# One core, two interleaved lanes: another table of turns for a two-layer decoder in fp32

## The chip, the cores and the metric

The kernel runs on one core of a Trainium2 chip. The metric is the device time of one execution in microseconds. The kernel before has a median of 643.53 us over 3 runs (643.41 to 644.73). The profiled execution is a separate one, of 639.99 us.

The core's engines each take their own list of instructions strictly in order and meet only at semaphores: PE (matmul), DVE (vector), ACT (activation functions and copies), POOL (elementwise, here softmax scaling and parts of the expert product) and SP (issues the DMAs).

## The reference

`x` is (4, 256, 128), the context `ctx` is (4, 256, 128), all fp32. Six pre-norm residual stages:

```python
x = x + L0_attn(layernorm(x))        # 16 heads of 8; attn = softmax(q k^T * 128**-0.5) + rel_bias; out = layernorm(attn v)*gamma + beta
x = x + L0_xattn(layernorm(x), ctx)  # 16 heads of 64, causal and padding mask, keys and values from ctx
x = x + L0_ffn(layernorm(x))         # 8-bit activations, ternary weights, 128 -> 512, conv over 3 tokens, silu, 512 -> 128
x = x + L1_attn(layernorm(x))        # grouped heads, causal, scores + slope*(j - i), softmax, projection
x = x + L1_xattn(layernorm(x), ctx)  # per token: softmax over the 16 heads of k against the 16 heads of q
x = x + L1_ffn(layernorm(x))         # 8 experts of 128, top 2, plus one shared expert

def swiglu(h):                       # in L1_ffn, a = swiglu(h1 * h3), y = a @ w2.T + b2, weighted by the router
    g = jnp.minimum(h[..., ::2], LIMIT)
    l = jnp.clip(h[..., 1::2], -LIMIT, LIMIT)
    return g * jax.nn.sigmoid(ALPHA * g) * (l + 1.0)
```

## The kernel before, in words

The four batches of 256 tokens are split in two lanes, A (batches 0 and 1) and B (batches 2 and 3). A lane has its own half of the on-chip memory, its own four PSUM banks (`A_banks`, `B_banks`) and its own tiles, so the lanes share no data but weights. Each lane does the six stages one after another. In names the stages are `l0a` (`rel_attention`), `l0x` (`cross_attention`), `ffn` (`quantized_ffn`), `l1a` (`alibi_attention`), `l1x` (`head_attention`) and `moe` (`expert_ffn`). `A_l0a_xn` is thus lane A's normalized x of the first stage.

A stage gives, for each engine, a Python generator: the code between two `yield`s emits a few instructions with their semaphore waits. `course()` strings a lane's six generators together for one engine. `merged()` then takes from the two lanes, and from two helper programs, by a string of turns: "A4 W1 A3" takes four pieces of lane A's program, one of W's, three of A's. W is `weight_levels()`, which rounds the ffn weights to their levels and multiplies two projection matrices; it works in lane B's memory before B starts. L (`late_loads()`) issues, on SP alone, the loads of the last two stages' weights. There is one string for each engine, in the table `TURNS`. So the strings fix how A's and B's instructions alternate in each engine's list; the order within a lane is fixed by the generators, and what waits for what by the semaphores.

The lines that the prediction speaks of:

- Stage `l0a`: L439 loads the context (SP); L608 transposes it (PE); L148 to L155 take the statistics of x and L164 normalizes it (DVE), L159 is the power -0.5 between them (POOL); L172 transposes the result (PE); L493 copies that out of PSUM (ACT); L622 projects one tile of 128 tokens to q, k, v (PE). q and k are split in three bf16 parts, L541 and L544 on DVE, L462, L465 and L471 on POOL, into a stack `expT` that L637 transposes (PE) and L434 copies to `qkT` (DVE). POOL's memsets L452 to L457 clear a lane's stack and value tiles. L226 makes scores for the row maximum (PE), L299 takes it (DVE, `nmax`). L323 and L327 and the DMA of L252 (`shiftT` into `qkT`) put the maxima into the queries; then L262 and L263 make the scores again (PE).
- Stage `l0x`: for a pair of heads L950 to L954 make scores (PE), L879 their maxima (DVE), L803 the exponentials (ACT), L966 transposes them (PE), L820 copies them (ACT), L979 multiplies by the values (PE).
- `l1a` also projects the context for `l1x` (L1518, L1523, PE).
- Stage `l1x`, once for each eighth of the tokens: L1707 and L1714 copy operands out of PSUM (ACT), L1742 and L1747 take maximum and difference (DVE), L1718 the exponential (ACT), L1759 the sum (DVE), L1830 the next products (PE).
- Stage `moe`, once per expert and lane: L2054 the two hidden products (PE), L1950 a bias add (ACT), L2021 to L2036 the clamped product (DVE), L1956 the sigmoid (ACT), L1926 and L1932 the products with router weight and gate (POOL), L2086 the output product (PE). L2007 and L2067 prepare router weights; L2046 adds the result to x at the end (DVE).

The sigmoid and the exponential of ACT lie in different function tables. An `ACT_TABLE_LOAD` stands in ACT's list wherever the next function needs another table than the last did; where that is depends on the order of the lanes' instructions.

The functions that make and use the table:

Of the kernel before, what the change touches and what calls it, by code (L numbers as in the profile page):

```python
# [2343 lines left out]
def course(lane, name, eng):  # L2344

    for st in lane.plan:
# [9 lines left out]

TURNS = {
    "tensor":
# [7 lines left out]
    "vector":  # L2366
# [8 lines left out]
    "scalar":  # L2375
# [4 lines left out]
    "gpsimd":  # L2380
        "A12 B3 A4 B13 A10 B2 A2 B3 A4 B1 A1 B1 A1 B1 A2 B1 A1 B2 A2 B1 A1 B7 A3 B2 A3 B2 A1 B8 A8 B3 A3 B3 A1 B1 A2 B3 A1 B2 A2 B2 A2 B1 A10 B4 A1 B10 A1 B2",
    "sync":
        "A1 W13 B1 A2 B2 L1 A6 L1 A3 B7 A1 B3 A2 B2 A1 B1",
}


# [153 lines left out]
```

## Time and profile before

| | before |
|---|---|
| median of 3 runs | 643.53 us |
| the profiled execution | 639.99 us |
| its span, first to last instruction | 638.0 us |
| PE busy | 542.6 us (85%) |
| DVE busy | 421.6 us (66%) |
| ACT busy | 327.5 us (51%) |
| POOL busy | 193.3 us (30%) |
| mean granted clock of PE | 0.946 of full |

The span is what the records cover; 1.99 us of the profiled time lie outside it. The busy time of an engine is the part of the span in which it executes something. No engine is busy throughout, so an average says little: for each stretch one has to see which engine has no gaps and, where all have, what each gap waits for. The profile's timeline gives for each row the start and the time in us, the operation with the tile it writes and those it reads, how many like it follow one another, and in brackets how long the engine was idle just before and what released it ("1.18 <-DVE A_l0a_qkT L434": idle for 1.18 us until the DVE instruction of L434 had written that tile). The granted clock tells which of its two levels, 1.2 and 2.4 GHz, PE ran at: 1.00 is 2.4 GHz, 0.50 is 1.2 GHz, and a value between them is a mean over time at either.

### The profile page before, as it was taken

To read this page: it belongs to the slowest core of one execution; us is meant where nothing else is said; L and a number is where in the kernel's file an instruction comes from. 1 tells how busy PE (TensorE), PEld (TensorE's weight loads), DVE (VectorE), ACT (ScalarE), POOL (GpSimd) and SP (SyncE) were. 2 spreads that over 40 slices of the span, in tenths; PEclk is the share of its full clock that TensorE was granted. 3 is DMA by queue.
4 is the path that set the end of the run, shared out by engine and by line. 5 is a ranking of instruction groups with operands and counts; after the bars stand their busy time and mean duration, and the time that the engine had idled before them with its cause. 6 is when DMAs were issued, how large, how long until landed. Compare 5 with 4: busy or idle time off the path is not lost. (4 is left out here: it accounts for less than half of the span.)

```text
span 638.0 us, 12873 instructions
## 1 busy us (share of the span) xinstructions
PE 542.6 (85%) x4890; PEld 334.9 (53%) x4890; DVE 421.6 (66%) x1037; ACT 327.5 (51%) x809; POOL 193.3 (30%) x288
## 2 busy tenths in 40 slices
PE   1777888999999999778896479988997989999995
PEld 1533344344555656455464355665665766655553
DVE  5595674642563554788559865757556567689894
ACT  1424355556577574586642535553664547363440
POOL 3554200312263443332620031001113122335663
PEclk9875799999999999889998789999998999999997
DMA  8600000000030000000166005300000000300301
GB/s 289 258 2 2 2 3 3 1 3 2 1 134 0 2 1 1 2 2 1 43 174 234 1 2 165 103 3 2 4 3 2 3 3 1 134 2 0 133 2 33
DMA packets 25815, 27.92 MB, mean 44 GB/s; under 512 B 18177, under 2 KB 22794, under 8 KB 24858
## 3 DMA queue, kind: packets, MB, share of 16 engines
q1 hardware_dynamic: 25754, 27.10, 12.7%
q8 instruction: 39, 0.64, 0.4%
q14 instruction: 22, 0.18, 0.1%
HBM read 22.14 MB, written 4.75 MB: 42 GB/s over the span
## 5 line engine op out<-in xcount | busy, mean ns | idle before, releaser
L785 POOL TENSOR_TENSOR A_l0x_prob<-A_l0x_prob,A_l0x_inverted_sums 128x256 f32<-128x256 f32 (+1 forms) x32 | 26.2, 840 | 61.7 <-DVE A_l0x_inverted_sums L896 61.7
L785 POOL TENSOR_TENSOR B_l0x_prob<-B_l0x_prob,B_l0x_inverted_sums 128x256 f32<-128x256 f32 (+1 forms) x32 | 27.1, 868 | 46.6 <-DVE B_l0x_inverted_sums L896 46.5
L879 DVE TENSOR_REDUCE A_l0x_nmax<-A_banks 128x2 f32<-128x256 f32 (+1 forms) x32 | 16.3, 551 | 26.9 <-PE A_banks L954 26.9
L2054 PE MATMUL A_banks<-A_moe_xT,w_moe_rows 128*128 128x512 f32 x72 | 34.0, 599 | 0.0
L2054 PE MATMUL B_banks<-B_moe_xT,w_moe_rows 128*128 128x512 f32 x72 | 33.3, 599 | 0.0
L299 DVE TENSOR_REDUCE B_l0a_nmax<-B_banks 128x2 f32<-128x512 f32 x32 | 21.4, 686 | 17.4 <-PE B_banks L226 17.3
L299 DVE TENSOR_REDUCE A_l0a_nmax<-A_banks 128x2 f32<-128x512 f32 x32 | 21.4, 685 | 12.0 <-PE A_banks L226 11.8
L333 ACT ACTIVATE A_l0a_expT<-A_banks 128x512 f32<-128x512 f32 x32 | 18.5, 599 | 21.0 <-PE A_banks L263 21.0
L803 ACT ACTIVATE B_l0x_prob<-B_banks,B_l0x_nmax 128x128 f32<-128x128 f32 x64 | 26.0, 421 | 6.0 <-DVE B_l0x_nmax L879 6.0
L803 ACT ACTIVATE A_l0x_prob<-A_banks,A_l0x_nmax 128x128 f32<-128x128 f32 x64 | 26.0, 427 | 1.2 <-DVE A_l0x_nmax L879 1.2
L820 ACT ACTIVATE B_l0x_probT<-B_banks 128x384 f32<-128x384 f32 x32 | 15.8, 493 | 21.0 <-PE B_banks L966 21.0
L333 ACT ACTIVATE B_l0a_expT<-B_banks 128x512 f32<-128x512 f32 x32 | 19.1, 604 | 14.3 <-PE B_banks L263 13.9
L820 ACT ACTIVATE A_l0x_probT<-A_banks 128x384 f32<-128x384 f32 x32 | 15.8, 493 | 15.8 <-PE A_banks L966 15.6
L333 ACT ACTIVATE A_l1a_expT<-A_banks 128x384 f32<-128x384 f32 x32 | 15.5, 493 | 16.2 <-PE A_banks L266 16.0
L1683 POOL TENSOR_TENSOR A_l1x_prob<-A_l1x_prob,A_l1x_rz 128x512 f32<-128x512 f32 x8 | 8.3, 1043 | 49.9 <-DVE A_l1x_rz L1764 49.9
L1950 ACT ACTIVATE A_moe_h<-A_banks,w_moe_rest_rows 128x512 f32<-128x512 f32 x18 | 12.3, 684 | 20.9 <-PE A_banks L2054 20.9
L333 ACT ACTIVATE B_l1a_expT<-B_banks 128x384 f32<-128x384 f32 x32 | 15.2, 493 | 13.0 <-PE B_banks L266 12.8
L879 DVE TENSOR_REDUCE B_l0x_nmax<-B_banks 128x2 f32<-128x256 f32 (+1 forms) x32 | 16.2, 547 | 8.3 <-PE B_banks L954 8.3
L299 DVE TENSOR_REDUCE B_l1a_nmax<-B_banks 128x2 f32<-128x512 f32 (+1 forms) x24 | 16.3, 685 | 7.3 <-PE B_banks L234 7.2
L1950 ACT ACTIVATE B_moe_h<-B_banks,w_moe_rest_rows 128x512 f32<-128x512 f32 x18 | 12.3, 682 | 15.4 <-PE B_banks L2054 15.3
L2054 PEld LDWEIGHTS B_banks<-B_moe_xT,w_moe_rows 128*128 128x128 f32 x72 | 12.6, 190 | 13.3 <-issue 10.3
L966 PE MATMUL B_banks<-w_const_rows,B_l0x_prob 128*128 128x128 f32 x96 | 17.2, 290 | 2.1 <-ACT B_l0x_probT L820 1.7
(610 smaller groups left out, 1605.1 us busy)
## 6 DMA issues: line engine op xcount, KB each, us to landing
w_toeplitz_rows<-in_toeplitz_rows SPq DMA_DIRECT2D x1, 3072.0 KB, 15.8
w_moe_rows<-in_moe_rows SPq DMA_DIRECT2D x1, 2304.0 KB, 8.8
w_l1x_rows<-in_l1x_rows SPq DMA_DIRECT2D x1, 2048.0 KB, 8.6
A_l1x_values<-A_l1a_v_tokens SPq DMA_DIRECT2D x4, 512.0 KB, 3.2
A_l1x_v_groups<-A_l1x_values SPq DMA_DIRECT2D x16, 128.0 KB, 3.1
B_l1x_values<-B_l1a_v_tokens SPq DMA_DIRECT2D x4, 512.0 KB, 3.4
B_l1x_v_groups<-B_l1x_values SPq DMA_DIRECT2D x16, 128.0 KB, 3.3
w_l0x_vo_rows<-in_l0x_vo_rows SPq DMA_DIRECT2D x1, 1024.0 KB, 8.9
```

The lines of the kernel that those rows point to most:

```text
L299: dve.tensor_reduce(out, scores, AX, ALU.max, negate=True).then_inc(self.s_mx.sem, 1)
L333: act.activation(self.expT[:, u % self.ring, :], self.exp_bank(u)[:, 0:self.W], ACT.Exp, scale=self.scale).then_inc(self.s_p.sem, 1)
L785: ins = pool.tensor_tensor(pair, pair, bcast(rz[:, g % 2, i, :], 2, n), ALU.mult)
L803: ins = act.activation(prob[:, u % RING, at:at + n], bank[u % 2][:, at:at + n], ACT.Exp, bias=nmax[:, b, i, h:h + 1], accum_out=zsum[:, g ...
L820: act.activation(probT[:, u % 4, :], bank[2][:, 0:W], ACT.Copy).then_inc(s_pt.sem, 1)
L879: ins = dve.tensor_reduce(nmax[:, b, i, 2 * c:2 * c + 2], lane.banks[:, 0:2, at:at + n], AX, ALU.max, negate=True)
L966: ins = pe.transpose(bank[2][:, c * P:(c + 1) * P], prob[:, u % RING, c * P:(c + 1) * P], w["ident"][:])
L1683: pool.tensor_tensor(pr, pr, bcast(rz[:, n % 2, :], BL, 64), ALU.mult).then_inc(s_pn.sem, 1)
L1950: act.activation(h1[:, n % 2, :], hidden_bank(2 * n)[:, :], ACT.Identity, bias=w["moe_b1"][:, e, part:part + 1]).then_inc(s_h1.sem, 1)
L2054: pe.matmul(hidden_bank(k)[:, :], w["moe_w3" if which else "moe_w1"][:, ORDER[i], part, :], xT[:], start=True, stop=True).then_inc(s_h.sem, 1)
```

## The change

All five strings of `TURNS` are replaced, and nothing else. The generators, the waits, the tiles and the number of PE, DVE, POOL and DMA instructions stay as they are. ACT's list has eight table loads in place of ten, since in two places the functions of one table now stand together. Two of the five strings, with their old forms:

```diff
     "gpsimd":
-        "A12 B3 A4 B13 A10 B2 A2 B3 A4 B1 A1 B1 A1 B1 A2 B1 A1 B2 A2 B1 A1 B7 A3 B2 A3 B2 A1 B8 A8 B3 A3 B3 A1 B1 A2 B3 A1 B2 A2 B2 A2 B1 A10 B4 A1 B10 A1 B2",
+        "A11 B1 A3 B1 A1 B1 A1 B13 A10 B1 A2 B3 A2 B1 A2 B1 A1 B1 A1 B1 A2 B1 A1 B2 A2 B1 A1 B6 A1 B2 A1 B1 A4 B2 A1 B8 A8 B2 A2 B2 A1 B2 A2 B2 A1 B3 A1 B1 A1 "
+        "B1 A1 B1 A5 B1 A6 B1 A1 B12 A1 B1 A1 B2",
     "sync":
-        "A1 W13 B1 A2 B2 L1 A6 L1 A3 B7 A1 B3 A2 B2 A1 B1",
+        "W4 A1 W9 B1 A2 B2 L1 A6 L1 A3 B5 A1 B5 A2 B2 A1 B1",
```

In SP's list the first DMA before is lane A's context (L439), ahead of the constants and of A's x. After, it is the seventh, right behind B's x.

On POOL, in the first stage, where lane A splits its third and fourth tile of q and k (L462 to L471) and lane B's part begins (L159 and the memsets), the order before is:

```order
L465 TENSOR_TENSOR A_l0a_split<-A_l0a_rest_qk,A_l0a_split 128x256
L471 COPY A_l0a_expT<-A_l0a_split 128x16x16 x2
L471 COPY A_l0a_expT<-A_l0a_split 128x16x8 x2
L159 TENSOR_TENSOR B_l0a_rstd<-B_l0a_ve,w_const_rows 128x4
L452 MEMSET B_l0a_expT 128x4x16x16
L453 MEMSET B_l0a_expT 128x4x16x13
L454 MEMSET B_l0a_expT 128x4x16x3
L455 MEMSET B_l0a_vals 128x3072
L457 MEMSET B_l0a_vals 128x64
L462 CAST A_l0a_split<-A_l0a_rest_qk 128x256
```

In the same place after the change:

```order
L465 TENSOR_TENSOR A_l0a_split<-A_l0a_rest_qk,A_l0a_split 128x256
L159 TENSOR_TENSOR B_l0a_rstd<-B_l0a_ve,w_const_rows 128x4
L471 COPY A_l0a_expT<-A_l0a_split 128x16x16 x2
L471 COPY A_l0a_expT<-A_l0a_split 128x16x8 x2
L462 CAST A_l0a_split<-A_l0a_rest_qk 128x256
L465 TENSOR_TENSOR A_l0a_split<-A_l0a_rest_qk,A_l0a_split 128x256
L471 COPY A_l0a_expT<-A_l0a_split 128x16x16 x2
L471 COPY A_l0a_expT<-A_l0a_split 128x16x8 x2
L452 MEMSET B_l0a_expT 128x4x16x16
L453 MEMSET B_l0a_expT 128x4x16x13
```

A's fourth tile now goes ahead of B's five memsets, and B's L159 ahead of the copies of A's third tile. On DVE, to match, the four L164 of B (`B_l0a_xn`) move from amid A's maxima L299 to between A's last L541 and L544, and A's first copy L434 moves ahead of the two last roundings of W (L2157, L2160).

On PE, where lane B goes through its last pairs of heads of `l0x` (L950 to L979) and lane A begins to project the context (L1518, L1523), the order before is:

```order
L966 MATMUL B_banks<-w_const_rows,B_l0x_prob 128x128 x3
L1518 MATMUL A_banks<-w_l1x_rows,A_ctxT 128x512
L1523 MATMUL A_banks<-A_ctxT,w_l1x_rows 64x256 x4
L950 MATMUL B_banks<-B_l0x_kT,B_l0x_qT 128x128 x2
L952 MATMUL B_banks<-B_l0x_kT,B_l0x_qT 128x256 x2
L954 MATMUL B_banks<-B_l0x_mask_q,w_ident_bf 128x384 x2
```

And after:

```order
L966 MATMUL B_banks<-w_const_rows,B_l0x_prob 128x128 x3
L950 MATMUL B_banks<-B_l0x_kT,B_l0x_qT 128x128 x2
L952 MATMUL B_banks<-B_l0x_kT,B_l0x_qT 128x256 x2
L954 MATMUL B_banks<-B_l0x_mask_q,w_ident_bf 128x384 x2
L966 MATMUL B_banks<-w_const_rows,B_l0x_prob 128x128 x3
L979 MATMUL B_banks<-B_l0x_probT,B_l0x_vals 64x256 x2
L979 MATMUL B_banks<-B_l0x_probT,B_l0x_vals 64x128 x2
L1518 MATMUL A_banks<-w_l1x_rows,A_ctxT 128x512
L1523 MATMUL A_banks<-A_ctxT,w_l1x_rows 64x256 x4
```

The first context projection of A now stands behind the scores and the value products of B's next pair.

On ACT, where lane A's first expert (sigmoid L1956) meets lane B's last eighths of `l1x` (exponential L1718), the order before is:

```order
L1956 ACT_TABLE_LOAD
L1956 ACTIVATE A_moe_sigmoid<-A_moe_gate 128x512
L1714 ACTIVATE B_l1x_probT<-B_banks 128x512
L1718 ACT_TABLE_LOAD
L1718 ACTIVATE B_l1x_prob<-B_l1x_prob 128x512
L1707 ACTIVATE B_l1x_keysT<-B_banks 128x4x128
```

After the change the loads stand in one place, behind B's last exponential:

```order
L1714 ACTIVATE B_l1x_probT<-B_banks 128x512
L1718 ACTIVATE B_l1x_prob<-B_l1x_prob 128x512
L1956 ACT_TABLE_LOAD
L1956 ACTIVATE A_moe_sigmoid<-A_moe_gate 128x512
L1950 ACTIVATE A_moe_h_165<-A_banks,w_moe_rest_rows 128x512 x2
L1707 ACTIVATE B_l1x_keysT<-B_banks 128x4x128
```

(`A_moe_h_165` is the tile `A_moe_h`.) Elsewhere many turns of one to three pieces are exchanged, on every engine. Over the last expert of both lanes the order on PE ends as before.

## Rows read from the trace of the kernel before

**Rows 1.** The page: busy time, share of the span and instructions by engine.

```profile
PE 542.6 (85%) x4890; PEld 334.9 (53%) x4890; DVE 421.6 (66%) x1037; ACT 327.5 (51%) x809; POOL 193.3 (30%) x288
```

**Rows 2.** Stretches: length, busy PE, PEld, DVE, ACT, POOL, granted clock, DMA share, GB/s.

```profile
60.00:80.00 20.00, 17.82 (x143) 7.98 (x140) 13.56 (x27) 7.77 (x20) 5.81 (x13) 0.74 0.01 2
600.00:620.00 20.00, 20.00 (x71) 10.36 (x70) 19.55 (x24) 8.54 (x14) 13.72 (x10) 1.00 0.00 1
0.00:638.00 638.00, 542.56 (x4890) 334.95 (x4890) 421.56 (x1037) 327.52 (x809) 193.32 (x288) 0.95 0.13 44
```

**Rows 3.** Timeline of the start: SP, DVE, PE.

```profile
0.74 0.45 SPq L439 DMA_DIRECT2D A_l0a_rest_qk<-in_ctx  x1
1.78 0.43 SPq L2217 DMA_DIRECT2D A_x<-in_x  x1
...
6.25 0.87 DVE L148 BATCH_NORM_STATS2 A_l0a_bn<-A_x 128x6 f32<-128x128 f32 x4 [6.25 <-DMA A_x<-in_x]
...
13.54 1.12 PE L172 MATMUL A_banks<-w_const_rows,A_l0a_xn 128*128 128x128 f32 x4 [8.08 <-DVE A_l0a_xn L164]
```

**Rows 4.** Timeline, DVE and PE, 20 to 24 us.

```profile
20.83 0.69 DVE L2157 TENSOR_SCALAR B_wq_r<-B_wq_r 128x1024 f32<-128x1024 f32 x1
21.55 0.77 DVE L2160 TENSOR_SCALAR w_ffn_q<-B_wq_r 128x1024 bf16<-128x1024 f32 x1
...
22.80 0.58 PE L637 MATMUL A_banks<-w_ident_bf,A_l0a_expT 128*128 128x128 bf16 x4 [1.18 <-DVE A_l0a_qkT L434]
```

**Rows 5.** Timeline of POOL, PE and DVE, 33 to 42 us; DVE at 555 us.

```profile
33.84 2.69 POOL L455 MEMSET B_l0a_vals<- 128x3072 f32 x1
...
39.15 0.61 PE L637 MATMUL A_banks<-w_ident_bf,A_l0a_expT 128*128 128x128 bf16 x4 [0.66 <-POOL A_l0a_expT L471]
...
39.28 2.09 DVE L164 TENSOR_SCALAR B_l0a_xn<-B_x,B_l0a_mv,B_l0a_rstd 128x128 f32<-128x128 f32 x4
...
555.93 1.11 DVE L164 TENSOR_SCALAR B_moe_xn<-B_x,B_moe_mv,B_moe_rstd 128x128 f32<-128x128 f32 x4 [0.90 <-POOL B_moe_rstd L159]
```

**Rows 6.** Timeline of PE, 51 to 57 us.

```profile
51.92 0.41 PE L262 MATMUL A_banks<-A_l0a_qkT 64*128 64x256 bf16 x2 [3.54 <-DMA A_l0a_qkT<-A_l0a_shiftT]
...
56.19 1.59 PE L622 MATMUL B_banks<-w_l0a_rows,B_l0a_xT 128*128 128x384 f32 x2
```

**Rows 7.** Timeline of PE and ACT, 302 to 309 us.

```profile
302.00 1.12 PE L1518 MATMUL A_banks<-w_l1x_rows,A_ctxT 128*128 128x512 f32 x2 [0.93 <-DVE A_x L1188]
303.05 1.08 PE L1523 MATMUL A_banks<-A_ctxT,w_l1x_rows 128*64 128x256 f32 x8
...
308.29 0.49 PE L950 MATMUL B_banks<-B_l0x_kT,B_l0x_qT 64*128 64x128 f32 x4 [1.26 <-ACT B_l0x_prob L803]
...
302.09 0.48 ACT L803 ACTIVATE B_l0x_prob<-B_banks,B_l0x_nmax 128x256 f32<-128x256 f32 x1
```

**Rows 8.** Timeline of ACT, DVE and PE, 530 to 554 us.

```profile
530.22 1.28 ACT L1956 ACT_TABLE_LOAD   x1
...
532.65 1.28 ACT L1718 ACT_TABLE_LOAD   x1
...
534.60 0.69 DVE L1759 TENSOR_REDUCE B_l1x_zsum<-B_l1x_prob 128x8 f32<-128x512 f32 x1 [1.62 <-ACT B_l1x_prob L1718]
...
544.05 1.28 ACT L1956 ACT_TABLE_LOAD   x1
...
553.62 1.05 PE L2086 MATMUL A_banks<-w_moe_w_rows,A_moe_a 128*128 128x128 f32 x8
```

**Rows 9.** Timeline of the experts: PE, DVE.

```profile
586.66 0.61 PE L2067 MATMUL B_banks<-w_const_rows,B_moe_expert_weight 128*9 128x128 f32 x4 [1.02 <-DVE B_moe_expert_weight L2007]
...
624.22 1.16 PE L2086 MATMUL B_banks<-w_moe_w_rows,B_moe_a 128*128 128x128 f32 x8 [0.63 <-POOL B_moe_a L1932]
...
592.39 0.69 DVE L2036 SCALAR_TENSOR_TENSOR B_moe_l1g<-B_moe_h,B_moe_gate 128x512 f32<-128x512 f32 x1
...
607.67 1.64 DVE L2036 SCALAR_TENSOR_TENSOR B_moe_l1g<-B_moe_h,B_moe_gate 128x512 f32<-128x512 f32 x1
```

41 rows, old and new, of the table TURNS are left out of this document.

## The prediction

> **What bounds the kernel now.** I read first the busy time by engine. PE works 542.6 of 638.0 us [rows 1], so 95 us of the span are gaps of PE, and its work can't be reordered away. Then the stretches of 20 us, to see where these gaps lie. In 600 to 620 us PE has none and DVE almost none (19.55 of 20); in 60 to 80 PE is at 17.82, with a clock of 0.74 [rows 2]. No engine is full elsewhere, so the time between is a chain that goes from engine to engine. The printed chain of what ended last reaches back only some 14 us and says nothing of the rest. I therefore went through the timeline of PE and, for every idle time in brackets, through the engine that it names: what stood ahead of the releasing instruction in that engine's list, and whether it belonged to the other lane. Only that can change here, for the work is the same. Where the order after puts the awaited instruction first, the gap shrinks by what is moved away, at most to zero; where the moved work was itself awaited, its lane pays.
>
> What a move gains counts for the end only if the next place of that lane, and then the other lane's, can use it. PE is busy 85% of the time, so most of what one lane gains is soon handed to the end; that is the weakest link of the sum, and rival 1.
>
> **Start, 0 to 14 us.** SP issues A's context first (0.45 us long, the next one 0.51 later), and A_x third, at 1.78 [rows 3]. DVE does nothing until A_x has landed, at 6.25, and PE's first transposes of the normalized x start at 13.54 after DVE [rows 3]. After the change A_x is issued one place earlier: 0.5 us. The context is wanted by PE ahead of 13.54 and is issued about 3 us later than before; its transfer then has until 13 us, about 9 us, so it costs nothing. Cover gone, it costs what it is late. Gain 0.5, bounds 0 (the transfers, not their issue, set the landing) and 0.54.
>
> **20 to 24 us.** PE waits 1.18 us for DVE's first L434, which stands behind L2157 (0.69) and L2160 (0.77) [rows 4]. After, it stands ahead of both. L434 could have begun when its scores were there, shortly after 21. Gain 0.75, bounds 0 and 1.4. The rounding is late instead, which only the ffn wants, more than 200 us later.
>
> **30 to 45 us.** Here A's fourth tile on POOL waits behind B's five memsets, one of them of 2.69; PE then waits 0.66 for A's L471 at 39.15, and DVE stops A's maxima for B's xn, 2.09 [rows 5]. After, the tile goes first and xn fills a time in which DVE was idle 0.5 to 0.6 us at 30 and at 31. So A's way to its last maximum loses the 0.66, and of the 2.09 what fits in idle time (1.1): 1.76. Against it xn now stands ahead of A's L544, and costs there between 1.11, the price of the same four instructions at 555.93, and 2.09 [rows 5], less the idle time it fills: 0.5 net. Gain 1.25, bounds from a loss of 1.0 (xn at full price on A's way, nothing back) to a gain of 2.75. The same xn at two prices, 2.09 beside POOL's long product and 1.11 at 555.93, is what this term hangs on.
>
> The Trainium skill has a rule for it ("SBUF — State Buffer", Who interferes with whom): a tensor_scalar in a mode that takes the second pair of ports, and POOL, lock each other out for a whole instruction. At its new place xn lies beside POOL's copies L471, so by that rule it would cost 2.09 there too, and the term would be 0.3; by the row at 555.93, where POOL does little, 1.25. The trace agrees that the price doubles beside POOL; which of the two holds at the new place no row shows.
>
> **50 to 82 us.** PE waits 3.54 us for the DMA of A's maxima, and at 56.19, at low clock, B's L622 (1.59) stands ahead of A's scores [rows 6]. One such L622 now fills part of the wait and the others go behind A's scores. A is ahead by 1.59, twice at most, 3.2; but B is behind by as much, and PE has gaps enough in this stretch (2.2 of 20 in rows 2) for only part. Gain 1.0, bounds 0 and 3.2; a loss is rival 2.
>
> **302 us.** ACT's L803 for B ends at 302.57 (302.09 and 0.48), and B's next scores L950 could follow. PE does A's L1518 and L1523 first, 1.12 and 1.08 [rows 7], until 304.06. B's pairs are a chain at that time: PE waits on B's L803 again at 308.29 for 1.26. After, A's two stand behind B's pair. Gain 304.06 less 302.57, 1.5; A's projection is wanted only by `l1x`. Bounds 0 and 2.8 (the same exchange on DVE and ACT some 40 us earlier, if these do not already lie in a gap).
>
> **336 to 372 us.** DVE holds this stretch, and both lanes' instructions change places by 1 to 2 us, B's forward and A's back. I take zero, bounds 1 either way.
>
> **530 to 546 us.** A's first sigmoid takes a table load at 530.22, B's exponential another at 532.65, each 1.28, and the next sigmoid a third at 544.05; DVE waits 1.62 for that exponential [rows 8]. After there is one load, behind B's last exponential. With two loads and the sigmoid, over 2.6 us, gone from ahead of the exponential, the whole wait goes. Gain 1.6 on B's chain. A's first sigmoid is later by some 12 us, but its product is wanted by PE's first L2086 only at 553.62 [rows 8], and A does other experts' L2054 meanwhile, so it costs nothing; without that cover it would eat the whole term. Bounds 0 and 2.2 (the load at 544.05 adds 0.5 where PE waits on ACT behind it).
>
> The Trainium skill ("ScalarE: Activation LUTs", What ACT_TABLE_LOAD costs) gives 1.28 us for the load, as here, and a drain of 1.38 behind it. Here the sigmoid starts at 531.51, right at the end of the load; so this trace shows no such drain behind it, and two loads fewer are worth 2.6, not 5.3.
>
> **The experts, 555 us to the end.** PE waits 1.02 for L2067 at 586.66 [rows 9]. After, three products of A's stand ahead of it, so this wait goes: 1.0. Against it POOL does one more L1926 of A between B's L1926 and L1932 at 622, ahead of the wait of 0.63 at 624.22 [rows 9]: 0.6 lost. Net 0.4, bounds a loss of 0.6 and a gain of 1.0. The last products, POOL's last three and the stores keep their order.
>
> **New waits.** Some hundred other exchanges on PE make none of the gains above and can only be neutral or make waits. I count three of the usual 0.5: a loss of 1.5.
>
> Sum: 0.5 + 0.75 + 1.25 + 1.0 + 1.5 + 0 + 1.6 + 0.4 = 7.0, less 1.5 = 5.5. The profiled execution took 639.99, with 1.99 outside its span, so I expect 634.5 of one like it; it lies 3.5 below the median of the runs, so the median becomes 643.53 less 5.5 = 638.0.
>
> **Rivals.**
>
> 1. *Given back.* Each gain ends at the next place where the lanes meet: in 600 to 620 us PE is full, and what comes before it may end there in a longer wait of the lane that was not helped. For it: the moves are local, and the order is back level within 20 to 40 us. Against: PE full at the end means that a lane which arrives earlier ends earlier. Time 643.5.
>
> 2. *Slower: B falls behind in 50 to 105 us.* After, B's instructions on PE stand behind up to 5.8 us more of A's work between 60 and 80 us, 3.4 on average (summing before's durations over both orders), and the order is level again only at 95 to 105. If B's part of the first stage is the later one, its chain (scores, maximum, DMA like the 3.54 at 51.92, exponentials) is not ready when PE's order comes to it, and PE waits. It decides from the point at which B's delay exceeds PE's gaps, 2.2 us in 60 to 80 [rows 2]. The price is 3.4 to 5.8 less these 2.2, so 1.2 to 3.6, 2.4 in the middle, and with xn at its full price (a loss of 1.0 in place of 1.25) and the other gains given back, 643.53 + 2.4 + 1 = 646.9.
>
> 3. *More than the sum.* Two things: the clock, at half speed for (1 - 0.946) x 638 / 0.5 = 69 us, may be granted otherwise when the gaps move; and DVE's L2036 costs 1.64 in eight of its instructions from 578 us on, 0.69 in the others [rows 9], so 0.95 each, 7.6 in all. If a third of the latter goes as the lanes' phase shifts, 2.5, and 3 us more of the upper bounds hold: 638.0 less 5.5 = 632.5. Both can as well go the other way, which the range takes in. The skill's page on SBUF (same section) says that a DVE instruction with two inputs there contends with a reading POOL; it agrees with the two prices.
>
> **Chances.** The forecast, 634.5 to 641.5: 0.56. Rival 1: 0.17, of which 0.11 within 0.2% (1.3 us, about what can be told from no change), 0.04 faster, 0.02 slower. Rival 2: 0.15. Rival 3: 0.12. So faster 0.72, same 0.11, slower 0.17. The range is 632 to 646: it leaves out half of rival 3, two thirds of rival 2. The forecast's own range is 634.5 to 641.5.
>
> **What would show it.** A_x lands 0.5 earlier; no 1.18 at 22; xn's four L164 ahead of L544, at 1.1 or 2.1; B's L622 behind A's scores; L950 of B right behind L803 at about 299; one table load between 525 and 545; no 1.02 ahead of L2067. B's gaps on PE between 70 and 105 larger by over 3 us would show rival 2 right and the forecast wrong, as would a span over 637.

## The result, and the profile after

| | before | after |
|---|---|---|
| median, first comparison (4 runs each) | 644.13 us | 619.22 us |
| ratio, with its 95% interval | | 0.9628 (0.9555 to 0.9701) |
| median, second comparison (23 and 6 runs) | 644.23 us | 621.69 us |
| ratio, with its 95% interval | | 0.9684 (0.9632 to 0.9736) |
| the profiled execution | 639.99 us | 625.54 us |
| its span | 638.0 us | 623.8 us |
| mean granted clock in it | 0.946 | 0.937 |
| idle time of PE in it, up to its last product | 91.8 us | 74.5 us |

The change is worth 22 to 25 us. I had forecast 5.5 (a median of 638.0, range 632 to 646): the direction was right, the size was wrong by a factor of four.

The ratios and the distances at equal clock leave out slow runs (over 1.5% above the fastest of their kernel) and the medians do not: that takes 6, 5 and 4 of 12 runs from three versions below, and with all its 12 the first DMAs alone would stand at -1.0 (0.4) in the table below, not at -2.3 (0.5).

The busy times by engine, on the page of the profile after, where [rows 1] stand for before:

```profile
PE 545.6 (87%) x4880; PEld 334.3 (54%) x4890; DVE 423.3 (68%) x1037; ACT 324.6 (52%) x807; POOL 192.8 (31%) x288
```

The stretch from 60 to 80 us as in [rows 2], and the one from 105 to 240 us (columns: length, busy time of PE, PEld, DVE, ACT, POOL, granted clock, DMA share, GB/s):

```profile
60.00:80.00 20.00, 16.79 (x134) 7.18 (x132) 12.89 (x30) 7.03 (x20) 6.26 (x14) 0.74 0.01 2
105.00:240.00 135.00, 132.15 (x973) 68.81 (x968) 74.36 (x210) 89.05 (x275) 45.85 (x62) 0.99 0.05 17
```

PE and DVE work no less than before: 545.6 us against 542.6, 423.3 against 421.6. ACT works 2.9 less, of which two table loads of 1.28 make 2.56. The time came out of PE's idle time, 17.2 us of it. PE's 3 us of more work go with a lower mean clock (0.937 against 0.946) in this execution. The gain must be looked for in many places.

The start, where [rows 3] stand for before (start and time in us, operation, idle time before it and what ended it):

```profile
1.20 0.42 SPq L2217 DMA_DIRECT2D A_x<-in_x  x1
...
3.63 0.51 SPq L439 DMA_DIRECT2D A_l0a_rest_qk<-in_ctx  x1
...
4.08 0.87 DVE L148 BATCH_NORM_STATS2 A_l0a_bn<-A_x 128x6 f32<-128x128 f32 x4 [4.08 <-DMA A_x<-in_x]
...
6.80 4.74 DVE L164 TENSOR_SCALAR A_l0a_xn<-A_x,A_l0a_mv,A_l0a_rstd 128x128 f32<-128x128 f32 x4
...
11.09 1.09 PE L608 MATMUL A_banks<-w_const_rows,A_l0a_rest_qk 128*128 128x128 f32 x4 [11.09 <-DMA A_l0a_rest_qk<-in_ctx]
11.96 1.06 PE L172 MATMUL A_banks<-w_const_rows,A_l0a_xn 128*128 128x128 f32 x4
```

A_x, lane A's input, lands at 4.08 us, not 6.25, though it is issued only 0.58 earlier. The context, issued at 3.63, becomes the last to arrive: PE's L608 waits for it until 11.09, and L172 follows at 11.96 (13.54 before).

The places of [rows 4 to 6], 20 to 57 us:

```profile
20.58 0.59 PE L637 MATMUL A_banks<-w_ident_bf,A_l0a_expT 128*128 128x128 bf16 x4 [0.18 <-DVE A_l0a_qkT L434]
...
28.36 1.24 DVE L164 TENSOR_SCALAR B_l0a_xn<-B_x,B_l0a_mv,B_l0a_rstd 128x128 f32<-128x128 f32 x4
...
28.27 1.22 POOL L471 COPY A_l0a_expT<-A_l0a_split 128x256 bf16<-128x256 bf16 x4
...
49.46 0.40 PE L262 MATMUL A_banks<-A_l0a_qkT 64*128 64x256 bf16 x2 [2.15 <-DMA A_l0a_qkT<-A_l0a_shiftT]
```

PE's wait for DVE's first L434 is 0.18 (1.18 before). B's xn costs 1.24 at its new place, although POOL's L471 runs beside it from 28.27 on. The wait for the DMA of A's maxima is 2.15 (3.54 before).

The places of [rows 7 to 9], 299 us and the last stages:

```profile
299.85 0.49 PE L950 MATMUL B_banks<-B_l0x_kT,B_l0x_qT 64*128 64x128 f32 x4 [1.36 <-ACT B_l0x_prob L803]
...
302.26 1.12 PE L1518 MATMUL A_banks<-w_l1x_rows,A_ctxT 128*128 128x512 f32 x2
...
525.18 1.28 ACT L1956 ACT_TABLE_LOAD   x1
...
516.53 0.69 DVE L1759 TENSOR_REDUCE B_l1x_zsum<-B_l1x_prob 128x8 f32<-128x512 f32 x1 [0.36 <-ACT B_l1x_prob L1718]
...
571.01 0.60 PE L2067 MATMUL B_banks<-w_const_rows,B_moe_expert_weight 128*9 128x128 f32 x4
...
610.00 1.16 PE L2086 MATMUL B_banks<-w_moe_w_rows,B_moe_a 128*128 128x128 f32 x8 [1.05 <-POOL B_moe_a L1932]
```

B's L950 stands ahead of A's L1518 and still waits 1.36 for ACT. There is one table load, at 525.18, until those of the router at 546. From 510 us on the longest wait of L1759 is 0.36; before, its waits there were 1.51, 1.28 and 1.62. L2067 waits for nothing. L2086 at the end of B's seventh expert waits 1.05 (0.63 before).

### The profile page after: what moved, and what is told of

The parts are those of the page before. It is cut to its first block and busy times, and to the rows that moved or that the text cites. A ratio compares the mean times of both kernels' runs of the same rounds, so it can differ in the third digit from the quotient of the medians.

```text
span 623.8 us, 12862 instructions
## 1 busy us (share of the span) xinstructions
PE 545.6 (87%) x4880; PEld 334.3 (54%) x4890; DVE 423.3 (68%) x1037; ACT 324.6 (52%) x807; POOL 192.8 (31%) x288
## 5 line engine op out<-in xcount | busy, mean ns | idle before, releaser
L299 DVE TENSOR_REDUCE B_l0a_nmax<-B_banks 128x2 f32<-128x512 f32 x32 | 21.9, 689 | 18.5 <-PE B_banks L226 18.4
L299 DVE TENSOR_REDUCE A_l0a_nmax<-A_banks 128x2 f32<-128x512 f32 x32 | 21.4, 688 | 13.6 <-PE A_banks L226 13.5
L333 ACT ACTIVATE A_l1a_expT<-A_banks 128x384 f32<-128x384 f32 x32 | 15.4, 495 | 12.5 <-PE A_banks L266 12.3
L1950 ACT ACTIVATE A_moe_h<-A_banks,w_moe_rest_rows 128x512 f32<-128x512 f32 x18 | 12.2, 682 | 18.1 <-PE A_banks L2054 18.1
L299 DVE TENSOR_REDUCE B_l1a_nmax<-B_banks 128x2 f32<-128x512 f32 (+1 forms) x24 | 16.2, 686 | 7.5 <-PE B_banks L234 7.3
L226 PE MATMUL A_banks<-A_l0a_qkT 64*128 64x256 bf16 x64 | 15.8, 356 | 4.4 <-DVE A_l0a_nmax L299 3.1
L299 DVE TENSOR_REDUCE A_l1a_nmax<-A_banks 128x2 f32<-128x512 f32 (+1 forms) x24 | 16.1, 687 | 5.1 <-PE A_banks L234 5.1
```

The source lines that it names most:

```text
L226: ins = pe.matmul(bank[:, c * S:(c + 1) * S], self.q(b, h, c * P, P), self.k(b, h, 0, S), start=(c == 0), stop=True, skip_group_check=True)
L299: dve.tensor_reduce(out, scores, AX, ALU.max, negate=True).then_inc(self.s_mx.sem, 1)
L333: act.activation(self.expT[:, u % self.ring, :], self.exp_bank(u)[:, 0:self.W], ACT.Exp, scale=self.scale).then_inc(self.s_p.sem, 1)
L1950: act.activation(h1[:, n % 2, :], hidden_bank(2 * n)[:, :], ACT.Identity, bias=w["moe_b1"][:, e, part:part + 1]).then_inc(s_h1.sem, 1)
```

## The experiments

**How they are made and read.** At a point at which the old and the new string of an engine have taken the same pieces from each lane, one can change from one string to the other. There are 452 such points on PE, 485 on DVE, 353 on ACT, 123 on POOL. So a kernel can have the new turns in one stretch, on all engines, and the old ones in the rest. I call such a point level. The stretches are named by the time of before's trace at which they begin and end. One engine's string is never exchanged by itself, as the order on one engine presupposes that on the others; what a single engine's order is worth was therefore not tried.

Two measures are given for each kernel. The first is the median of its runs and the ratio to before. Its intervals are 0.3 to 0.7% either way, too wide for single terms, as the mean granted clock of a run goes from 0.926 to 0.957 in all kernels and the time with it. One slope fits them all: 4.5 us for 0.01 of clock, with 1.2 us of scatter around it (66 runs of before, 5 to 12 of each other kernel, those out of both comparisons for the whole table). The second measure is therefore the distance to before at equal clock, by that fit, with its standard error in brackets. It has a limit: where an order itself brings more or less low clock, the fit takes that out as if it were chance. A third look is free of noise: between places where only the order differs, and no low clock falls, the distance of the same instruction in two traces stays within 0.02 us for over a hundred us. I call this distance the lead over before.

| new turns in | median (us) | ratio (95% interval) | us at clock 0.940, less before |
|---|---|---|---|
| 0 to 105 us | 642.06 | 0.9986 (0.9950 to 1.0022) | -2.6 (0.4) |
| 0 to 240 us | 634.69 | 0.9886 (0.9840 to 0.9932) | -8.8 (0.5) |
| 0 to 400 us | 629.32 | 0.9796 (0.9747 to 0.9846) | -11.9 (0.5) |
| 0 to 500 us | 625.34 | 0.9712 (0.9663 to 0.9761) | -15.4 (0.6) |
| all | 621.69 | 0.9684 (0.9632 to 0.9736) | -20.2 (0.4) |
| the first DMAs alone | 642.61 | 0.9945 (0.9892 to 0.9998) | -2.3 (0.5) |
| all but the first DMAs | 624.68 | 0.9718 (0.9654 to 0.9782) | -18.6 (0.5) |
| 105 to 240 us alone | 636.55 | 0.9881 (0.9835 to 0.9928) | -5.9 (0.4) |
| 298 to 309 us alone | 640.55 | 0.9965 (0.9935 to 0.9995) | -1.3 (0.4) |
| 525 to 560 us alone | 641.46 | 0.9946 (0.9906 to 0.9986) | -1.7 (0.5) |
| 560 us to the end alone | 641.02 | 0.9971 (0.9940 to 1.0003) | -1.4 (0.4) |
| all, context issued fourth | 620.53 | 0.9648 (0.9602 to 0.9693) | -20.3 (0.5) |

At equal clock before is at 642.4 us.

### Where the gain lies: four growing parts

The edits, as numbers of pieces of the string that are taken from the new table, counted from its start:

```diff
-tensor   0 of 840   vector   0 of 950   scalar   0 of 546   gpsimd   0 of 156   sync  0 of 47
+tensor 151 of 840   vector 176 of 950   scalar  71 of 546   gpsimd  32 of 156   sync 17 of 47   # p105
+tensor 346 of 840   vector 357 of 950   scalar 235 of 546   gpsimd  61 of 156   sync 19 of 47   # p240
+tensor 528 of 840   vector 595 of 950   scalar 342 of 546   gpsimd  93 of 156   sync 35 of 47   # p400
+tensor 717 of 840   vector 790 of 950   scalar 461 of 546   gpsimd 107 of 156   sync 41 of 47   # p500
```

Up to 105 us. Expected:

> The new turns only up to 105 us of the old timeline (the first stage), the old ones behind. Theory E (early): most of the 25 us come from the first stage, where the lanes are put in another phase: 630 us or less, ratio 0.98 or lower. Theory L (late): the first stage gives about my forecast's 3.5 us for it and the rest comes behind: 640 to 644, ratio 0.995 to 1.00.

Measured: a median of 642.06, and -2.6 at equal clock. Theory E falls.

Up to 240 us. Expected:

> The new turns up to 240 us of the old timeline. Theory E: 628 or less. Theory L: in the two profiles the lanes are level with before (within 1 us) at 200 to 250 us, so 641 to 645, ratio 0.995 to 1.002. A third one, C (clock): the profile of after ran the first 120 us at a lower clock than its other runs did, and the new turns win 8 us there in those: 633 to 637.

Measured: 634.69, 6.1 us beyond the first part at equal clock. Theory L had expected nothing here, theory C 8 us by the clock. The gain is there at equal clock, so it is the order's. The profile of after had hidden it by more low clock at its start: 0.79 on the mean up to 105 us, where that of before had 0.85.

Up to 400 and up to 500 us. Expected:

> The new turns up to 400 us. Theory E: 622 to 628. Theory L: in the profile after leads by 6 us at 400, so 636 to 639, ratio 0.99. C: 8 more than that, 628 to 631.

> The new turns up to 500 us; the old ones in the rest (the end of l1x and the experts). Theory E: 620 to 625. Theory L: the profile of after leads by 10.5 us at 500 and ends 14.2 ahead, so 631 to 635; the rest of 4 to 10 us comes from the last 140 us, the two table loads among them. C: 624 to 627.

Measured: 629.32 and 625.34, another 3.1 and 3.5 at equal clock; the rest, from 500 us on, brings 4.8. The medians fit C's numbers, which came from the sum of all, better than its reason. So the gain is spread over the whole program: 0.025 us per us up to 105, 0.045 from 105 to 240, 0.02 from 240 to 400, 0.035 behind.

What such a part consists of is seen in the PE waits between 105 and 240 us, of 0.2 us and more (what PE waited for; us in total, times, longest). In the kernel with new turns up to 105 us:

```profile
PE B_banks L286 <- DVE B_l0a_xn L587: 1.3, 1, 1.3
PE A_banks L966 <- DVE A_l0x_qT L836: 0.9, 1, 0.9
PE A_banks L930 <- ACT A_l0x_probT L820: 0.6, 2, 0.4
PE A_banks L966 <- ACT A_l0x_probT L820: 0.6, 1, 0.6
PE B_banks L950 <- ACT B_l0x_prob L803: 0.4, 2, 0.2
PE B_banks L966 <- DVE B_l0x_qT L836: 0.4, 1, 0.4
```

And in the one with new turns up to 240 us:

```profile
PE A_banks L966 <- ACT A_l0x_probT L820: 0.7, 1, 0.7
PE B_banks L286 <- DVE B_l0a_xn L587: 0.2, 1, 0.2
PE B_banks L226 <- DVE B_l0a_nmax L299: 0.2, 1, 0.2
```

Eight waits of 0.2 to 1.3 us become three of 0.2 to 0.7. The part's work, from the level point at its start to the one at its end, takes 146.7 us in the first and 141.5 in the second, 5.2 less. PE's idle time in it falls from 7.2 to 3.8, so 3.4 of these are waits that the records show. The other 1.8 us lie in time that counts as busy: 139.5 and 137.7 us for the same products at the same mean clock (0.99). No line holds much of it (L680 of B 3.4 and 3.2, L930 of B 6.8 and 6.6). The ends of products in the profile are modelled, and neighbouring ones overlap, so a short wait can hide between two of them; that this is where the 1.8 lie is my reading and not shown. The lead grows in many steps up and down, not in one place.

### Additive or joint: one part alone

```diff
-tensor 151 to 346, vector 176 to 357, scalar 71 to 235, gpsimd 32 to 61 of the old table
+the same pieces of the new table (old ones ahead and behind)   # s105_240
```

> The new turns only between 105 and 240 us of the old timeline, a stretch to which I gave nothing. Behind a new first stage it brought 5.2 us in the trace at equal clock and 7.4 in the medians. Theory A (additive: each stretch removes its own waits, whatever stands ahead): 636 to 638, and a lead of 3 to 5.5 us at 240 us, reached in steps of 0.4 to 1.2. Theory J (joint: it only pays off the debt of 1.8 that the new first stage leaves lane B with at 105): 640 or more, a lead of 3 or less.

Measured: 636.55, -5.9 at equal clock, against 6.1 as the second part behind a new first one. In its trace the lead goes from -3.8 at 95 us to +1.4 at 240, by 5.2, as in the other pair, though the lanes come to it in the old phase. PE's idle time falls from 6.9 to 3.4 in it, and its busy time by 1.7, again as in the other pair. Theory A holds.

### The whole table again

```diff
-all five strings old
+all five strings new   # full_again
```

> The whole new table once more, as a measure beside the partial ones. From the runs so far, at equal mean clock (0.936 to 0.937) before takes about 644.5, the table up to 105 us 641, to 240 635, to 400 632, to 500 629, the whole 625.5. Theory K (order alone): the median lies at 619 to 626, and at equal clock the distance to before is 17 to 20 us, as PE's idle time fell by 17.2 us in the traces (91.6 to 74.4). Theory F (clock too): the new table is also granted a higher clock on the average, and the median stays at 617 to 620, 25 below before.

Measured: 621.69, and at equal clock -20.2 for the ten runs of both comparisons. So K: the order alone is worth 20 us. The mean clock of these runs is 0.9433 against 0.9396, which makes 1.7 us more by the slope. That the new order is granted the higher clock, and isn't only lucky in ten runs, is not shown: theory F stays open.

### The first DMAs

```diff
-        "A1 W13 B1 A2 B2 L1 A6 L1 A3 B7 A1 B3 A2 B2 A1 B1",
+        "W4 A1 W9 B1 A2 B2 L1 A6 L1 A3 B7 A1 B3 A2 B2 A1 B1",   # sp_start; after_old_sp: the same on the new table, turned round
```

> The old table but for the order of the first DMAs: A's context is issued seventh, as in the new table, not first. My forecast was 0.5 us. The traces show A_x landing at 4.08 in place of 6.25, and PE's L172 at 11.96 in place of 13.54. Theory S (kept): the first rows of the trace lead by 1.6 to 2.2 us, and the lead reaches the end at full size, 641 against 643, since the old order behind it waits for the same things. Theory G (given back): the lead is gone by 105 us, and the time is that of before.

> The new table, but with the old order of the first DMAs (A's context first). Theory S: 1.6 to 2.2 us above the whole new table, all along from the first rows on. Theory G: level with it from 105 us on.

Measured: -2.3 alone, and 1.5 (0.6) lost when it is taken out of the new table. In the trace of the one with the first DMAs alone:

```profile
4.05 0.87 DVE L148 BATCH_NORM_STATS2 A_l0a_bn<-A_x 128x6 f32<-128x128 f32 x4 [4.05 <-DMA A_x<-in_x]
...
10.68 1.09 PE L608 MATMUL A_banks<-w_const_rows,A_l0a_rest_qk 128*128 128x128 f32 x4 [10.68 <-DMA A_l0a_rest_qk<-in_ctx]
...
299.76 1.12 PE L1518 MATMUL A_banks<-w_l1x_rows,A_ctxT 128*128 128x512 f32 x2 [0.93 <-DVE A_x L1188]
```

A_x lands 2.20 earlier, and L1518 of [rows 7] starts at 299.76, not 302.00: the lead is 2.24, and it stays between 2.04 and 2.26 on both lanes and every engine from 15 to 340 us. Behind that, stretches of low clock fall at other places in the two traces, and at the end the lead is 1.5. So theory S is shown up to 340 us, and the runs at equal clock (-2.3) say the same of the end. Only 0.6 us of the earlier landing is the issue (1.20 in place of 1.78), the other 1.6 the transfer, with the 256 KB of the context now behind A_x and not ahead of it.

The first stage as a whole is worth 2.6, so my three other terms in it, 3.0 together, come to 0.4 (0.6). In the kernel with new turns up to 105 us, lane A leads by 5.8 at 70 to 80 us (2.2 of it the start's), lane B by 0.8, and both by 1.0 from 108 on. The waits ahead of that, on PE:

```profile
100.48 0.28 PE L226 MATMUL B_banks<-B_l0a_qkT 64*128 64x256 bf16 x1 [0.57 <-DVE B_l0a_nmax L299]
101.66 0.39 PE L226 MATMUL B_banks<-B_l0a_qkT 64*128 64x256 bf16 x2 [0.29 <-DVE B_l0a_nmax L299]
102.84 0.39 PE L226 MATMUL B_banks<-B_l0a_qkT 64*128 64x256 bf16 x2 [0.79 <-DVE B_l0a_nmax L299]
```

B's maxima, which A's lead had put off, are awaited there: 0.57, 0.29 and 0.79. This is rival 2's mechanism at the place it named, at a price of 1.65. But it is not why the terms are gone. PE has done the same work at 89.72 us of before and 86.06 of this trace, and again at 109.12 and 108.16: the lead goes from 3.7 to 1.0. These stretches are, before and with the new turns:

```profile
89.72:109.12 19.40, 16.06 (x205) 9.06 (x202) 9.78 (x28) 12.13 (x25) 0.00 (x0) 1.00 0.01 3
86.06:108.16 22.10, 18.75 (x205) 9.17 (x204) 10.74 (x30) 12.11 (x25) 0.00 (x0) 0.92 0.01 3
```

PE idles 3.3 us in both, as waits of A's L680 and L286 went when B's came (3.2 before, 1.5 now). The 2.7 us lost lie in its busy time, 16.06 and 18.75 for the same products, and a stretch at 1.2 GHz falls into the second only. All eight traces that have the new first stage have a granted clock of 0.91 in 100 to 120 us, and all six that have the old one 1.00. That is 1.7 us at most; the other 1.0 is not explained. The fit at equal clock takes such a cost out, so the first stage may be worth less than its 2.6: without the correction its runs average only 0.2 below those of before. What makes the clock fall there was not tried.

### The named places by themselves

298 to 309 us, all engines, 3 exchanges on PE:

```diff
 L966 MATMUL B_banks<-w_const_rows,B_l0x_prob 128x128 x3
-L1518 MATMUL A_banks<-w_l1x_rows,A_ctxT 128x512
-L1523 MATMUL A_banks<-A_ctxT,w_l1x_rows 64x256 x4
 L950 MATMUL B_banks<-B_l0x_kT,B_l0x_qT 128x128 x2
...
+L1518 MATMUL A_banks<-w_l1x_rows,A_ctxT 128x512
+L1523 MATMUL A_banks<-A_ctxT,w_l1x_rows 64x256 x4
```

> The new turns only between 298 and 309 us of the old timeline, where A's first L1518 and L1523 are put behind B's next pair of heads. My forecast was 1.5 (L950 of B right behind its L803, not behind the two). Theory P (place by place, as the sums at equal clock show elsewhere): a constant lead of 1 to 1.5 us from 309 us on, and as much at the end. Theory Q (the gap only moves: A's two stand in B's next wait anyway): a lead under 0.6.

Measured: -1.3 (0.4), and in the trace a lead of 0.6:

```profile
303.19 0.49 PE L950 MATMUL B_banks<-B_l0x_kT,B_l0x_qT 64*128 64x128 f32 x4 [1.65 <-ACT B_l0x_prob L803]
...
305.61 1.13 PE L1518 MATMUL A_banks<-w_l1x_rows,A_ctxT 128*128 128x512 f32 x2
...
308.15 0.49 PE L950 MATMUL B_banks<-B_l0x_kT,B_l0x_qT 64*128 64x128 f32 x4
```

Before, PE waited 0.93 at L1518 and 1.26 at the next L950, 2.19 in all; now 1.65 at the first L950 and nothing at the second. That is Q's mechanism at a size just beyond it, while the runs say P: A's two products had stood for the most part in a wait for ACT anyway.

525 to 560 us:

```diff
-L1956 ACT_TABLE_LOAD
-L1956 ACTIVATE A_moe_sigmoid<-A_moe_gate 128x512
 L1714 ACTIVATE B_l1x_probT<-B_banks 128x512
-L1718 ACT_TABLE_LOAD
 L1718 ACTIVATE B_l1x_prob<-B_l1x_prob 128x512
```

> The new turns only between 525 and 560 us, where the first sigmoid of A goes behind B's last exponential and two table loads go. My forecast was 1.6. The trace gives 1.2 (5.8 less a lead of 7.0 for the steps from 525 to 560 in the new table). Theory P: a constant lead of 1.2 to 1.6 from 560 on. Theory W (the wait for the loads was hidden behind DVE): 0 to 0.5.

Measured: -1.7 (0.5). The loads in its trace and the wait behind them:

```profile
532.95 0.62 ACT L1718 ACTIVATE B_l1x_prob<-B_l1x_prob 128x512 f32<-128x512 f32 x1
...
542.25 1.28 ACT L1956 ACT_TABLE_LOAD   x1
...
533.61 0.69 DVE L1759 TENSOR_REDUCE B_l1x_zsum<-B_l1x_prob 128x8 f32<-128x512 f32 x1 [0.37 <-ACT B_l1x_prob L1718]
```

The exponential runs with no load ahead of it, DVE's wait for it is 0.37 (1.62 before), and the one load stands at 542.25. A stretch of low clock falls at 528 us of this trace, and at about the same instructions in four others with the old order there, which lose 1.7 of their lead by it. This one loses 0.6, so the new turns give 1.1 in the trace, a little under theory P's 1.2, and far from W.

From 560 us on:

```diff
-tensor 763 to 840, vector 862 to 950, scalar 501 to 546, gpsimd 126 to 156 of the old table
+the same pieces of the new table   # s560_640
```

> The new turns only from 560 us on. My forecast was 0.4 (1.0 won at L2067, 0.6 lost at POOL's L1926). At equal clock, the whole of 500 to the end is worth 4.9 us. Theory P: what 500 to 560 does not give, so 1 to 2.5. Theory D (phase: the new order from 560 on only gains where the stretch ahead hands it the lanes in another phase): 0.5 or less alone.

Measured: -1.4 (0.4), within P; in the trace the lead goes from 0.4 at 555 us to 1.2 at the end, so by 0.8. L2067 waits for nothing (1.02 before). Against it B's two last L2086 wait 1.05 and 1.40 in place of 0.63 and 0.83. So both of my two parts are there, and the waits in the records do not fall at all in sum: the 0.8 lie in busy time, as in 105 to 240 us. With 1.7 for 525 to 560, the stretch from 500 to 525, to which I gave nothing, is left with 1.7 (0.9).

### A version beyond both

```diff
-        "W4 A1 W9 B1 A2 B2 ...
+        "W2 A1 W11 B1 A2 B2 ...   # after_ctx5: the context is the fourth DMA
```

> A version that should beat both: the new table, with A's context issued fourth in place of seventh, still behind A's x. In the trace of the new table PE waits for that context until 10.67 to 11.09 us, while the first tiles of xn are there. If the context lands 1.5 us earlier and A's x is not slowed, L608 is out of the way and L622 can begin 0.4 us earlier: 0 to 0.6 faster than the new table. If the context shares its bandwidth with A's x again, 0 to 1 slower.

Measured: 620.53, and 621.69 for the new table in the comparison before, at equal clock 0.1 (0.6) apart: no difference that these runs can tell. In its trace, against the second trace of the new table, L608 runs at 7.08 in place of 10.67 and L622 at 13.08 in place of 13.38, a lead of 0.3 that holds till 30 us, where the clocks part. A_x lands at 4.16, so it is hardly slowed by a context issued 1.0 behind it. PE now waits 2.35 for the two last tiles of A's xn, and not for the context: the four L164 take 4.38 us beside POOL's memsets L452 to L455, and B's took 1.11 at 555.93.

## Why the prediction was wrong

**The start.** Forecast 0.5 with 0.54 as the upper bound, measured 2.3 (0.5), in the trace 2.2. The bound was wrong, not only the value: I priced a place in SP's queue and took the transfer as fixed. Its row was there: 4.5 us from the issue of A_x to its landing with a load of the same size ahead of it. The context's later issue, which I said costs nothing, costs 0.3 in the trace.

**20 to 24, 30 to 45, 50 to 82 us.** Forecast 3.0, measured 0.4 (0.6). Each wait behaved as I said (L434's 1.18 became 0.18, xn cost 1.24 and not the 2.09 beside POOL's long product, the DMA wait fell by 1.4). The new turns up to 400 us have the same first stage, and a trace with as much low clock in it up to 90 us as that of the first DMAs alone; there they lead the latter by 2.5 (84.95 against 87.46 us for the point at 89.72 of before), near the forecast of 3.0. By 109 us it is gone again. B's late maxima, rival 2's mechanism at the low end of its price, are there, but other waits went as they came; 1.7 at most goes with a stretch of low clock that every trace of the new first stage has, and the rest is open. I had no term for either. The rule of the Trainium skill ("SBUF — State Buffer", Who interferes with whom) would have had xn cost 2.09 beside POOL's copies; it ran at 1.24 beside them, so the measurement decides for the row at 555.93, at this place.

**302 us.** Forecast 1.5, measured 1.3 (0.4), in the trace 0.6. **336 to 372 us.** Forecast 0, not run by itself; with the new turns up to 240 us PE idles 18.1 us between 327 and 377 us, with those up to 400 us 17.0 over the same products, so within my bounds of 1 as far as idle time tells. **530 to 546 us.** Forecast 1.6, measured 1.7 (0.5), in the trace 1.1; the sigmoid again starts right at the end of the load (525.18 and 1.28, then 526.48), so no drain behind it shows here either. **The experts.** Forecast 0.4, measured 1.4 (0.4), in the trace 0.8; the two waits I named are both in the trace. In that of the whole new table DVE's L2036 at 1.64 became rarer, 6 of 18 against 8 of 18, as rival 3 had it. Together these places brought 7.1 of the 7.0 that I had given them: their errors cancel, which is luck, and none of them explains a factor of four.

**New waits.** This is the step that failed: "Some hundred other exchanges on PE make none of the gains above and can only be neutral or make waits. I count three of the usual 0.5: a loss of 1.5." Measured, the stretches in which I had named nothing gained: 6.1 us from 105 to 240, about 1.8 from 240 to 400 without the place at 302, 3.5 from 400 to 500, 1.7 from 500 to 525. That is 13 of 20 us, where I had 1.5 lost: the whole error of the sum. I had priced a gap only where I could name the move that ends it, and taken every other exchange for neutral. In the trace of before PE has 32 gaps of 0.9 us and more; 22 are left after. Ahead of the same products, the gaps of 1.27 us at 142.7, 1.12 at 311.9, 1.90 and 1.95 at 349.9 and 352.4, 1.04 at 433.1 and 0.97 at 479.7, none of which stands in my sum, became 0.23, 0, 0.07, 0.76, 0 and 0: 7.2 us in six. Others only shrank (1.58 at 339.6 to 1.02, 1.20 at 485.9 to 0.98), and the 1.00 at 288.3 grew to 2.42. By size, the gaps under 1 us were 39.9 us in 93 and are 34.4 in 102, those of 1 to 2 us were 27.5 in 21 and are 16.0 in 13, the six longer ones 24.3 and 24.2. And in 105 to 240 us, the stretch that gained most, PE had only 4.5 us of idle time before; a third of its gain lay in time that the records count as busy. I had used the full 20.00 of PE in such slices as a sign that nothing could be won there. It isn't one.

**Rival 1**, given back, holds for lane A's lead in the first stage alone. A lead of both lanes was kept to 0.02 us wherever order and clock were the same, the start's 2.24 from 80 to 340 us. In these traces only a lead of one lane over the other was lost. That distinction was missing in my weakest link, as I called it.

## What to carry to other kernels

Where strictly ordered queues of several engines are interleaved, a gain that moved all lanes was kept as far as the traces can be compared (340 us), and one that moved a lane ahead of the other was mostly gone at the next level point: price the two apart. When a change moves hundreds of small things, sum the whole of the bottleneck's idle time by size and by stretch before reading single rows (92 us here, of which the change took 17), and let the range reach to a share of that sum. Even that is no upper bound for a stretch: 105 to 240 us gained more than its 4.5 us of idle time. Price the order in which loads are issued by what stands ahead of the first one that is awaited (2.2 us here), not by the issue alone (0.6).

## What the runs showed that was not expected

- The time of a run follows its mean granted clock with 4.5 us per 0.01, over 0.926 to 0.957, for every version; the profile of before (0.946) was a run above its average (0.9396), and that alone accounts for 2.9 of the 3.5 us by which it lay under the median.
- Here a 256 KB load ahead of another delayed its landing by 1.6 us beyond the 0.6 of its issue.
- Traces of different kernels are the same to 0.02 us over 150 us and more where order and clock are the same. Two single profiles so tell a change of 0.3 us in place, where 6 to 12 runs at equal clock tell some 1.0 (two standard errors).
- The same four L164 took 1.11 us at 555.93, 1.24 beside POOL's copies L471, 2.09 beside POOL's products and 4.38 to 5.13 beside POOL's memsets at the start.
